# A recommender kernel: single rows, upper layers and block answers one step later, first-layer dense parts computed in steps 5 to 7

## The reference

```python
x = layer_norm(dense_t @ Wd.T, gd, bd)
y = layer_norm(jnp.einsum('bnd,ed->bne', sparse_t, Ws), gs, bs)
y = jnp.einsum('bne,pn->bep', y, Wsi)
y = layer_norm(y, gsi, bsi)
y = jnp.swapaxes(y, 1, 2)
T = jnp.concatenate([x[:, None, :], y], axis=1)
Z = jnp.einsum('bnd,bmd->bnm', T, T)
Zflat = Z[:, TRIL_I, TRIL_J]
out = layer_norm(Zflat @ Wl.T, gl, bl)      # 512 wide, the first 384 are used
...
h = jnp.concatenate([z, r_dense_t], axis=1)  # 384 + 256
h = jnp.maximum(h @ W_top1 + b_top1, 0.0)    # first MLP layer, 512 wide
h = jnp.maximum(h @ W_top2 + b_top2, 0.0)    # 256 wide
y = h @ W_top3
```

## Time and profile before

| | |
|---|---|
| profiled execution, its own time | 204.47 us |
| its span | 202.7 us |
| mean granted TensorE clock | 0.899 |
| TensorE matmuls busy | 155.0 us (76%) |
| VectorE busy | 116.8 us (58%) |
| GpSimd busy | 102.9 us (51%) |
| ScalarE busy | 85.2 us (42%) |
| DMA | 12.01 MB, mean 59 GB/s |

### The profile page before, as it was taken

The page is one execution under the profiler, slowest core; times in us unless marked ns, Lnnn a source line. Parts: engine busy times, 40 slices in busy tenths (PEclk is TensorE's granted clock), DMA queues, the critical chain, the costliest instruction groups (busy, mean ns, idle before and its releaser), DMA issues.

```text
span 202.7 us, 4648 instructions
## 1 busy us (share of the span) xinstructions
PE 155.0 (76%) x1865; PEld 106.3 (52%) x1865; DVE 116.8 (58%) x279; ACT 85.2 (42%) x229; POOL 102.9 (51%) x108
## 2 busy tenths in 40 slices
PE   0547787597806995599699939987995999496996
PEld 0435354463302683266497725657883464395684
DVE  2896239876828259819754990779099358600000
ACT  2002317735351193527526650546476034712063
POOL 3787777777777777777787777771000000000000
PEclk9995569889985699799999997999999699889999
DMA  5514132151935122312135241121411101152000
GB/s 143 173 27 129 32 124 81 25 186 37 269 67 76 28 58 37 57 26 55 28 73 65 52 69 26 29 55 44 53 32 18 31 0 31 32 63 36 0 3 0
DMA packets 38521, 12.01 MB, mean 59 GB/s; under 512 B 34114, under 2 KB 35266, under 8 KB 38499
## 3 DMA queue, kind: packets, MB, share of 16 engines
q1 hardware_dynamic: 34354, 8.26, 18.8%
q0 software_dynamic: 3328, 3.41, 8.3%
q10 hardware_dynamic: 816, 0.02, 0.2%
HBM read 9.46 MB, written 2.23 MB: 58 GB/s over the span
## 4 chain that ended last, share of the span: by engine, by line
PE 35%; POOL 16%; DMA 12%; DVE 11%; issue 9%; ACT 8%; SPq 7%; ACTq 0%; DVEq 0%
POOL rows L295 16%; PE pU L373 7%; DMA zscr<-zs 7%; PE pV L334 6%; PE pA L318 4%; SPq L235 3%; PE pU L414 3%; DVE t L768 2%; DVE evar L747 2%; DVE prod L744 2%; PE pU L400 2%; PE pA L373 2%; DMA z<-zscr 2%; PE pA L311 2%; ACT t L574 2%
## 5 line engine op out<-in xcount | busy, mean ns | idle before, releaser
L295 POOL DMA_INDIRECT rows<-in_tables,idx x104 | 102.7, 988 | 34.3 <-issue 31.4
L744 DVE TENSOR_TENSOR prod<-pA,rows 128x384 f32<-128x384 f32 (+1 forms) x16 | 9.4, 590 | 42.7 <-PE pA L318 42.6
L373 PE MATMUL pU<-wg,zr 128*128 128x512 f32 x24 | 17.4, 865 | 9.6 <-DMA z<-zscr 6.1
L334 PE MATMUL pV<-wexp,srow 128*64 128x192 f32 (+4 forms) x256 | 23.6, 335 | 0.7 <-DVE srow L759 0.7
L783 DVE TENSOR_TENSOR T<-t,trs 128x512 f32<-128x512 f32 x32 | 22.2, 694 | 1.1
L574 ACT ACTIVATE t<-t 128x512 f32<-128x512 f32 x32 | 19.5, 629 | 5.8 <-DVE t L768 5.7
L334 PEld LDWEIGHTS pV<-wexp,srow 128*64 128x64 f32 x256 | 17.7, 156 | 6.5 <-issue 2.7
L557 ACT COPY rowsT<-pA 128x384 f32<-128x384 f32 (+1 forms) x16 | 7.9, 497 | 31.0 <-PE pA L311 30.9
L318 PE MATMUL pA<-gbd,rowsT 128*128 128x128 f32 x104 | 18.7, 327 | 2.9 <-ACT rowsT L557 2.7
L768 DVE TENSOR_TENSOR t<-pT,bias 128x512 f32<-128x512 f32 x32 | 20.5, 683 | 0.4 <-PE pT L344 0.4
L774 DVE TENSOR_REDUCE tss<-t 128x16 f32<-128x512 f32 x32 | 20.4, 677 | 0.1
(11 more groups left out here) (153 smaller groups left out, 203.2 us busy)
## 6 DMA issues: line engine op xcount, KB each, us to landing
zscr<-zs SPq DMA_DIRECT2D x16, 128.0 KB, 2.0
rows<-in_tables,idx POOLq DMA_INDIRECT x104, 2.5
wl_sb<-in_wl SPq DMA_DIRECT2D x5, 256.0 KB, 2.7
w_sb<-in_w SPq DMA_DIRECT2D x5, 256.0 KB
dense_sb<-in_dense_t SPq DMA_DIRECT2D x1, 512.0 KB, 4.6
w_sb<-in_w SPq DMA_DIRECT2D x1, 512.0 KB, 6.3
zr<-zscr SPq DMA_DIRECT2D x4, 96.0 KB
zr<-zscr SPq DMA_DIRECT2D x4, 72.0 KB
```

Of the source, the lines that this page charges most:

```text
L295: pool.indirect_dma_start(out=rows[:, j, h * D:(h + 1) * D], out_offset=None, in_=tables, in_offset=bass.IndirectOffsetOnAxis(ap=idx[:, 2 ...
L334: got = mm(pV[(n - m + u) % 2][D * h:D * (h + 1), PJ * (a - US * u):PJ * (z + 1 - US * u)], srow[:, n % 2, i, D * h:D * (h + 1)], wexp[:, ...
L373: mm(upper_bank(k)[:], zr[:].rearrange("p a (g j) -> p (a g) j", j=4)[:, :, j], wg[:, j, :], start=j == 0, stop=False)
L744: v.tensor_tensor(prod[:, 0:count, :], pA[n % 2][:, 0:P * count].rearrange("p (j r) -> p j r", r=P), rows[:, first:first + count, :], ALU. ...
```

## The change

Weight loads are released one to two steps earlier; s_rows goes to steps 2 and 3 (single_rows stays in step 4, a step after s_rows); U0, U1, MLP, TOP and ANS come one step later; block 2's upper layer goes to steps 15 and 16. For blocks 0 to 2 the dense half of the first MLP layer is computed on its own in steps 5, 6 and 7 (dense_part), copied by ScalarE to hd (dense_kept), and added by VectorE (hidden_sum) to what hidden1 leaves in PSUM; relu1 reads that sum. hidden_bias writes to the end of bank pZ, ahead of interact(3), and is copied by ScalarE. For the last block the first batch of reads takes two units at its second unit, the second batch two at its fourth.

```diff
@@ -152,6 +152,9 @@
 h1 = sb("h1", [P, H1 // P, P])
+hd = sb("hd", [P, NBLK - 1, H1])
+hs = sb("hs", [P, H1])
+b1d = sb("b1d", [P, H1 // P])
 h2 = sb("h2", [P, H2 // P, P])
@@ -192,7 +195,8 @@
     sem, ["bias_done", "bias_sb", "beye_ready", "wb_done", "wb_sb", "wrow_done", "w9_ready", "w_ready", "wlm_sum", "gg_ready", "w9_sum", "w9_mean", "w9c_ready"])
-w1_ready, b1_done, b1_ready = map(sem, ["w1_ready", "b1_done", "b1_ready"])
+w1_ready, b1_done, b1_sb, b1_ready, hd_done, hd_sb, hs_sb = map(
+    sem, ["w1_ready", "b1_done", "b1_sb", "b1_ready", "hd_done", "hd_sb", "hs_sb"])
 gathered = [sem(f"gathered{i}") for i in range(NU)]
@@ -208,7 +212,7 @@
 LAST = NBLK - 1
-U0, U1, MLP, TOP, ANS = UNITS + 2, UNITS + 3, UNITS + 4, UNITS + 5, UNITS + 6
+U0, U1, MLP, TOP, ANS = UNITS + 3, UNITS + 4, UNITS + 5, UNITS + 6, UNITS + 7
 READS = 12
@@ -226,6 +230,10 @@
+def ahead(k):
+    return UNITS - 2 if k == LAST else UNITS - 1
@@ -250,13 +258,13 @@
     for j in range(NL):
-        if j % 2 == 0:
-            sp.wait_ge(r_done, 1 + j // 2)
+        if j % 3 == 0:
+            sp.wait_ge(r_done, 1 + j // 3)
         sp.dma_start(wl_sb[:, j, :], wl[:, j, :]).then_inc(ld_wl[j], 16)
...
         if c % 3 == 0:
-            sp.wait_ge(r_done, 4 + c // 3)
+            sp.wait_ge(r_done, 3 + c // 3)
         first = P * c if P * c < USED else P * c + UO - USED
@@ -269,18 +277,19 @@
         sp.dma_start(zscr9[k % 2, m], zs[:, n % 2, 4 * QG * G8:]).then_inc(zw[n % 2], 16)
-        if m == UNITS - 2:
+        if m == ahead(k) - 1:
             sp.wait_ge(zw[n % 2], 32 * (n // 2 + 1))
...
                 sp.wait_ge(u_done, k)
-            products(sp, k, range(0, UNITS - 1))
-            singles(sp, k, range(0, UNITS - 1))
+            products(sp, k, range(0, m + 1))
+            singles(sp, k, range(0, m + 1))
         if m == UNITS - 1:
             sp.wait_ge(zw[n % 2], 32 * (n // 2 + 1))
-            products(sp, k, range(m, UNITS))
+            sp.wait_ge(zw[(n - 1) % 2], 32 * ((n - 1) // 2 + 1))
+            products(sp, k, range(ahead(k), UNITS))
             if k < LAST:
-                singles(sp, k, range(m, UNITS))
+                singles(sp, k, range(ahead(k), UNITS))
     sp.wait_ge(o_sb, NBLK)
@@ -351,6 +360,8 @@
             pe.wait_ge(zs_sb, n)
+        if n == 4:
+            pe.wait_ge(b1_sb, 1)
         for g in range(G8):
@@ -366,6 +377,7 @@
             if k == 0:
+                pe.wait_ge(hd_sb, NBLK - 1)
                 pe.wait_ge(w_ready, NL)
@@ -384,37 +396,41 @@
-    def hidden1_dense(k):
-        if k < LAST - 1:
-            pe.wait_ge(zT_sb, k + 1)
+    def dense_part(k):
+        if k == 0:
+            pe.wait_ge(ld_w1, 16 * NK)
+            pe.wait_ge(w9_ready, 1)
         else:
-            pe.wait_ge(t1_sb, 2 * NU)
-        if k == LAST:
-            pe.wait_ge(zs_sb, NU)
-            pe.wait_ge(u_sb, LAST)
+            pe.wait_ge(hd_sb, k)
+        for m in range(H1 // P):
+            for c in range(USED // P, NK):
+                got = mm(pU[:, P * m:P * (m + 1)], w1_sb[:, c, P * m:P * (m + 1)],
+                         dense_sb[:, c - USED // P, P * k:P * (k + 1)], start=c == USED // P, stop=c == NK - 1)
+        got.then_inc(hd_done, 1)
+    def dense_last():
+        pe.wait_ge(t1_sb, 2 * NU)
+        pe.wait_ge(zs_sb, NU)
+        pe.wait_ge(u_sb, LAST)
+        for m in range(H1 // P):
+            for c in range(USED // P, NK):
+                mm(hidden_part(LAST, m), w1_sb[:, c, P * m:P * (m + 1)],
+                   dense_sb[:, c - USED // P, P * LAST:P * (LAST + 1)],
+                   start=c == USED // P, stop=False, skip_group_check=True)
+    def hidden1(k):
+        pe.wait_ge(zT_sb, k + 1)
         if k == 0:
             pe.wait_ge(w1_ready, 1)
-        for c in range(USED // P, NK):
-            for m in range(H1 // P):
-                mm(hidden_part(k, m), w1_sb[:, c, P * m:P * (m + 1)], dense_sb[:, c - USED // P, P * k:P * (k + 1)],
-                   start=c == USED // P and (m == 0 or k == LAST), stop=False, skip_group_check=True)
-    def hidden1(k):
-        pe.wait_ge(zT_sb, k + 1)
-        if k == LAST:
-            for m in range(H1 // P):
-                for c in range(USED // P):
-                    got = mm(hidden_part(k, m), w1g[:, c, P * m:P * (m + 1)], znT[:, c, :],
-                             start=False, stop=c == USED // P - 1, skip_group_check=True)
-                got.then_inc(h1_done, 1)
-        else:
+        if k == LAST - 1:
+            pe.wait_ge(t1_sb, 2 * NU)
+        for m in range(H1 // P):
             for c in range(USED // P):
-                for m in range(H1 // P):
-                    got = mm(hidden_part(k, m), w1g[:, c, P * m:P * (m + 1)], znT[:, c, :],
-                             start=False, stop=c == USED // P - 1, skip_group_check=True)
-                    if c == USED // P - 1:
-                        got.then_inc(h1_done, 1)
+                got = mm(hidden_part(k, m), w1g[:, c, P * m:P * (m + 1)], znT[:, c, :],
+                         start=c == 0 and k != LAST, stop=c == USED // P - 1, skip_group_check=k == LAST)
+            got.then_inc(h1_done, 1)
@@ -464,10 +480,9 @@
         pe.wait_ge(ld_w1, 16 * NK)
-        pe.wait_ge(w9_ready, 1)
         for m in range(H1 // P):
             for c in range(USED // P):
-                got = mm(pU[:, m:m + 1], w1_sb[:, c, P * m:P * (m + 1)], col["bl"][:, c:c + 1],
+                got = mm(pZ[:, ZF + m:ZF + m + 1], w1_sb[:, c, P * m:P * (m + 1)], col["bl"][:, c:c + 1],
                          start=c == 0, stop=c == USED // P - 1)
@@ -498,8 +513,10 @@
             x_turned()
+        if n == 7:
+            dense_part(2)
         if n == NU:
-            upper(LAST - 1, [4])
+            upper(LAST - 1, [2])
         if n:
@@ -508,15 +525,21 @@
             answer(k)
+        if n == 5:
+            pe.wait_ge(zs_sb, n - 2)
+            hidden_bias()
         if n >= 2:
             interact(n - 2)
+        if n == 2:
+            s_rows(range(0, 3))
         if n == 3:
-            s_rows(range(0, 3))
+            s_rows(range(3, NL))
         if n == 4:
-            s_rows(range(3, NL))
             single_rows()
         if n == 5:
-            hidden_bias()
+            dense_part(0)
+        if n == 6:
+            dense_part(1)
         if (k := block_at(n, TOP)) is not None:
@@ -524,18 +547,14 @@
         if (k := block_at(n, MLP)) is not None:
-            hidden1_dense(k)
             hidden1(k)
-        if n == NU - 2:
-            upper(LAST - 1, [0, 1, 2])
         if n == NU - 1:
-            upper(LAST - 1, [3])
+            upper(LAST - 1, [0, 1])
         if n == NU:
-            upper(LAST - 1, [5])
+            upper(LAST - 1, [3, 4, 5])
     interact(NU - 1)
-    hidden1_dense(LAST - 1)
     turn(LAST - 1)
-    hidden1_dense(LAST)
+    dense_last()
     hidden1(LAST - 1)
@@ -618,13 +637,25 @@
+    def dense_kept(k):
+        act.wait_ge(hd_done, k + 1)
+        a.copy(hd[:, k, :], pU[:]).then_inc(hd_sb, 1)
+    def bias_kept():
+        act.wait_ge(b1_done, 1)
+        a.copy(b1d[:], pZ[:, ZF:ZF + H1 // P]).then_inc(b1_sb, 1)
...
         for m in range(H1 // P):
-            if m == 0 or k == LAST:
-                act.wait_ge(h1_done, H1 // P * k + (m + 1 if k == LAST else H1 // P))
-            a.activation(h1[:, m, :], hidden_part(k, m), ACT.Relu, bias=b1p[:, m:m + 1]).then_inc(h1_sb, 1)
+            if k == LAST:
+                act.wait_ge(h1_done, H1 // P * k + m + 1)
+                got = hidden_part(k, m)
+            else:
+                act.wait_ge(hs_sb, k + 1)
+                got = hs[:, P * m:P * (m + 1)]
+            a.activation(h1[:, m, :], got, ACT.Relu, bias=b1p[:, m:m + 1]).then_inc(h1_sb, 1)
@@ -676,6 +707,8 @@
             mixed(n - 1)
+        if n in (6, 7):
+            dense_kept(n - 6)
         if (k := block_at(n, MLP)) is not None:
@@ -696,13 +729,17 @@
             interactions(n - 2)
-        if n in (1, 2, 3):
-            weight_sums(range(2 * n - 2, min(2 * n, NL)))
+        if n == 5:
+            bias_kept()
+        if n in (1, 2):
+            weight_sums(range(3 * n - 3, min(3 * n, NL)))
         if n in (4, 5):
...
             centred_rows()
-        if (k := block_at(n, U0)) is not None:
+        if n == 7:
+            dense_kept(2)
+        if (k := block_at(n, U0 - 1)) is not None:
             x_row(k)
@@ -716,7 +753,8 @@
     act.wait_ge(zw[(NU - 1) % 2], 32 * ((NU - 1) // 2 + 1))
-    singles(act, LAST, range(UNITS - 1, UNITS))
+    act.wait_ge(zw[NU % 2], 32 * ((NU - 2) // 2 + 1))
+    singles(act, LAST, range(ahead(LAST), UNITS))
     relu1(LAST - 1)
@@ -826,8 +864,15 @@
     def hidden_bias():
-        dve.wait_ge(b1_done, 1)
-        v.tensor_tensor(b1p[:], pU[:, 0:H1 // P], col["b1"], ALU.add).then_inc(b1_ready, 1)
+        dve.wait_ge(b1_sb, 1)
+        v.tensor_tensor(b1p[:], b1d[:], col["b1"], ALU.add).then_inc(b1_ready, 1)
+    def hidden_sum(k):
+        dve.wait_ge(h1_done, H1 // P * (k + 1))
```

(10 more changed lines are left out.)

## The result

The changed kernel takes 194.05 us (median of four, 192.37 to 195.35) against 204.69 before in the same comparison: ratio 0.949, interval 0.934 to 0.963. I had forecast 185.4 with a range of 179.5 to 194.0. So it is faster, as forecast, but by 10.6 us, not 19.3.

A forecast was written before the change was run, and what follows sets the result against it. The prediction took a chain of waits before single_rows, then TensorE's stalls at upper layers, as the bound. Transposes(15) at 141.7 plus a 41.9 tail gave 183.6 us of span, with 1.8 outside 185.4 us; range 179.5 to 194.

The forecast's parts named there:

- the gain from the lags: Later upper layers, hidden layers and answers: three stalls, 9.6 us together, removed, each with about 1.9 us of slow matmuls.
- the tail: From transposes(15) to the end: 41.9 us forecast against 40.67 before, ended by SyncE's queue behind u_done.
- the start's hole: 7.81 us of TensorE idle before single_rows, put first on a 5.97 us zscr write queued behind weight loads.
- Start: Up to transposes(5): 56.3 us instead of 64.36, 8.1 us off, then set by the gathers.
- Steps 5 and 6: Steps gaining dense_part(0) and dense_part(1): 9.8 and 7.4 us forecast, against 9.65 and 13.75 before.
- Step 7: Step with dense_part(2), its upper layer waiting for dense_kept(2): 13.3 us forecast against 6.90 before.
- Steps 8, 9, 10: Upper half 7.1 us, hidden1 9.2 and hidden2 7.6, the z read no longer late.
- Rival C: New waits for hd_sb and hs_sb replace the three stalls; only the start gains: 196.4 us, chance 0.10.
- the three stalls: TensorE's idles before upper layers, put on late z reads: 9.6 us together, each bringing about 1.9 us of slow matmuls.
- Steps 11 to 14: Two upper halves of 7.1 us each, hidden1 9.2 and hidden2 7.6, reaching transposes(15) at 141.7.
- A (gather-bound): Rival: transposes(15) sits on the gather floor of 139.0 us; 181.5 us in all, or 179.5; chance 0.20.
- D: Rival: TensorE, its holes gone, is held at 1.2 GHz, slower than before, up to 219 us; chance 0.04.

The follow-up runs named there:

- second profile: A second profiled execution of the unedited changed kernel: span 192.4 us, time 194.27 us, ratio 0.963 to the kernel before.
- loads alone: The kernel before with only the earlier release of the weight loads: ratio 1.001 (0.990 to 1.013).
- start alone: The kernel before with earlier loads, s_rows in steps 2 and 3 and weight sums in steps 1 and 2: ratio 0.986 (0.977 to 0.995).
- first profile: The profiled execution of the unedited changed kernel in the first comparison (median 194.05 us, ratio 0.949), 1.5% above the fastest execution there.
- kernel with early copies: The changed kernel with dense_kept(2) and the answer copies put ahead of ScalarE's squares: 188.48 us, ratio 0.935.
- GpSimd's reads: The changed kernel with the last block's reads of units 0 and 1 issued by GpSimd instead of SyncE: median 192.03 us, no interval.
- fastest form: The changed kernel with dense parts in place, the answer's copy ahead of the squares and units 0 and 1 read by GpSimd: 184.33 us, ratio 0.912.

## Why the prediction was wrong

The direction was right, and so was the gain from the lags. The sum was 8.8 us short of the second profile (183.6 against 192.4 of span). The step that failed most is the tail, 41.9 for 46.0: its path was right and its terms too small. Three others failed: the cause given for the start's hole, step 5, in which gram(5)'s wait for ScalarE and the fallen clock of dense_part(0) were put at nothing, and the wait for the answer's copy in step 11, which is not in the sum. By its own steps:

- **Start, forecast 8.1 us off, found 6.6** (transposes(5) at 57.8). The missing 1.5 us are the gathers' pace: the last gather of step 5 is issued at 54.78 instead of 53.78, and transposes(5) starts 3.0 us behind that, not 2.5. I had named contention with the loads and taken 0. The Trainium skill's rule (DMA: Bandwidth & Descriptors, Issuing engines are not separate DMA queues) would have put 1.3 us in, and transposes(4) at 49.7 against 48.5 looks like it; but the loads alone leave transposes(4) at 48.2, so that the loads are the cause is not shown. And the cause of the hole that I put first was hardly one: without the wait for the write (loads alone) 1.1 us is gained. What closes the hole is the order of s_rows and wbraw, with the weight sums moved beside it (start alone).
- **Steps 5 and 6, forecast 17.2, found 18.2** (20.5 in the first profile). Step 5 failed, 11.6 for 9.8. TensorE idles 1.23 us ahead of gram(5), since ScalarE's three centrings in step 4 now hold turned_rows(5), and dense_part(0) takes 3.23 us for 2.05, its clock fallen. Step 6 gives 0.8 back. I had also written that a late interact(3) matters to nobody before step 7. ScalarE takes its work in order and waits for it, 0.6 us in the first profile and 2.46 with dense_part(0) first, and its centring and turned_rows(6) stand behind. VectorE's two copies of the single rows, which I left out, come before row_variance(5), at 63.67, in VectorE's timeline of the second profile:

```profile
60.63 0.69 DVE L821 TENSOR_TENSOR T<-t,trs 128x512 f32<-128x512 f32 x1
...
62.24 0.69 DVE L857 COPY w<-pU 1x512 f32<-1x512 f32 x1
62.95 0.70 DVE L858 COPY w<-pU 1x512 f32<-1x512 f32 x1
63.67 0.56 DVE L782 TENSOR_TENSOR prod<-pA,rows 128x384 f32<-128x384 f32 x1
```

That is 5.9 us behind transposes(5); the prediction gives it no time of its own in step 5, and 2.4 in steps 10 and 14. In this profile TensorE is just as late at gram(6), so it costs nothing there; with hidden_bias taken out of step 5 it is what gram(6) waits for, 2.9 us. The kernel with the start alone shows such a wait too (1.8 us).
- **Step 7, forecast 13.3, found 12.7**, by the waits named, 2.40 of them for dense_kept(2). Right.
- **Steps 8, 9, 10, forecast 23.9, found 24.6.** Right. Rival C's waits exist, but the three stalls are gone beside them. One of the three was misread: the idle ahead of upper(0) ended with ScalarE's copy x_row(0), not with the z read, as TensorE's timeline of the kernel before has it:

```profile
83.42 4.42 PE L373 MATMUL pU<-wg,zr 128*128 128x512 f32 x6 [3.57 <-ACT z L601]
```

One step more covers that copy as well.
- **Steps 11 to 14, forecast 31.0, found 33.2**: 1.6 of it in step 11, where upper(1) waits 1.06 us for the answer's copy (o_sb), queued behind ScalarE's squares. Before, the wait for z had covered that copy. I asked of each engine what it would be late for and not of this semaphore. The kernel with early copies shows it: 7.5 us for the step.
- **Tail, forecast 41.9, found 46.0.** The largest miss. The mechanism (SyncE's queue behind u_done, then a fallen clock) was right, four sizes were small: u_done at +14.95 for +12.9, of which 1.3 is again the answer's copy, now of block 1, in step 15; the six reads 4.6 for 4.2; the doubled last reads 3.95 for 3.5; and the slow matmuls +3.0 for +1.8. My bound of 1.9 was taken from three matmuls where here four could be slow, and it set 4.59 us from the timeline against 2.6 from the chain; in the timeline the three take 2.94 at the upper clock. GpSimd's reads took 2 us off the start of upper(3) in the trace.

The errors of the four steps (start, 5 and 6, 11 to 14, tail) are 1.5, 1.0, 2.2 and 4.1 us and nearly all have one sign: where I had to fill in a wait I mostly took it as covered. A (gather-bound) failed for the changed kernel; in the fastest form transposes(15) starts 4.1 us after the last gather is issued, and one step waits 0.5 us for gathers. D did not occur as a loss: steps 7 to 14 were granted 1.00. But its sign, a granted clock of 0.50 with TensorE full, stands in step 5 for about 2 us. The agreement of step 7 and of steps 8 to 10 is good to 0.7 us; that the start and steps 5 and 6 come so near owes something to the profile chosen, since in the first one step 5 alone is 2.2 us longer. What stays open: why the first gathers lose 2 us in some executions, why the clock falls in some traces and not in others behind the same work, and whether the tail could start earlier by another order of u_done's own matmuls, which was not tried.

## What to carry to other kernels

When a stall is taken away, walk every semaphore of the instruction that waited, not only the one that came last: the next one may have been hidden by it (here the answer's copy, 1.1 to 1.3 us in two places, and ScalarE's centring at the start). Work that is moved "into free time" of one engine brings copies and waits on two others; here the dense part cost 3.6 us more where it was moved than where it was. And a copy that TensorE waits for belongs ahead of work that only the next step needs: two such copies moved up gave 5.9 us, about 0.9 of it not theirs by the trace; even so it is about half of what the whole change gave.

## What the runs showed of the hardware

The granted clock fell to 1.2 GHz (0.50) not only after idle time. In the changed kernel TensorE is busy throughout hidden_bias (24 matmul instructions with one output column) and interact(3) (64 of 34 columns), and dense_part(0) behind them takes 3.2 us instead of 2.05; where it stood before them it took 2.02. Two stretches of the second profile, gram(5) to interact(3) and then dense_part(0):

```profile
60.93:66.32 5.39, 5.39 (x99) 4.45 (x99) 5.21 (x11) 1.70 (x6) 4.01 (x5) 1.00 0.61 74
66.32:69.34 3.02, 3.02 (x23) 3.02 (x17) 1.75 (x3) 2.99 (x9) 2.27 (x3) 0.60 0.34 71
```

The kernel with hidden_bias in step 3 shows the same after a longer busy stretch. Its rows are step 3 up to hidden_bias, hidden_bias itself, then transposes(4) and mix(3).

```profile
40.77:47.02 6.25, 6.21 (x98) 3.37 (x98) 5.37 (x12) 3.63 (x11) 4.73 (x5) 1.00 0.73 215
47.02:50.35 3.33, 3.33 (x25) 3.33 (x25) 3.23 (x8) 0.61 (x2) 2.44 (x3) 0.80 0.41 79
50.35:53.39 3.04, 3.04 (x18) 1.95 (x18) 1.26 (x3) 0.59 (x1) 2.33 (x3) 0.50 0.13 25
```

It does not always happen: with dense_part(0) first, the stretch behind hidden_bias was granted 1.00.

A hole in front of wide matmuls can have a price of its own: after 4.8 us of idle the first eight matmul instructions of upper(3) took 6.8 us, after 1.5 us 3.82. The length of the idle does not give the price: after 1.85 us they took 5.52, after 2.0 (the kernel before) 3.82, after 4.84 5.86. The Trainium skill (TensorE: Matmul & The Clock Gate, HAM oscillation — how this bites in real kernels) tells of the clock falling when a wait for data parts groups of matmuls; the tail agrees, 6.8 us against 3.82.
